# Graph attention on one core: the reference maximum from row tiles 0 to 3, exponents in four groups, source scores negated on the way to PSUM, wh stored in four pieces

## The chip, the cores and the metric

One NeuronCore of a Trainium2 chip runs the whole program in one launch. The metric is the time of one execution on the device in microseconds (us). The core has a matrix engine (PE, TensorE), a vector engine (DVE, VectorE), an activation engine (ACT, ScalarE), a general one (POOL, GpSimd) and SP (SyncE), which here only issues transfers. Each engine runs its own list of instructions in order; engines meet at semaphores.

## The reference, cut to what matters

```
h  = max(layernorm(x), 0);   x1 = x + smooth(adj) @ h        # x: 2048 x 512
h2 = max(layernorm(x1), 0)
Wh = einsum('nf,hfd->hnd', h2, W)                            # 8 heads of 64 columns
e_src = sum(Wh * a1, -1);    e_dst = sum(Wh * a2, -1)        # one score per head and row
e  = leaky_relu(e_src[:, :, None] + e_dst[:, None, :], 0.2)
e  = where(adj > 0, e, -9e15);   att = softmax(e, axis=-1)
h  = elu(att @ Wh);   out = x1 + four dense layers(h)
```

The kernel does not form the exponent of every pair. exp(leaky_relu(s+d)) is one of two products, exp(s)exp(d) or exp(0.2 s)exp(0.2 d), by the sign of s+d. So it multiplies 0/1 matrices by Wh scaled with A = exp(d - top) and C = exp(0.2 (d - top)): q holds the neighbours with d >= -s, mask all neighbours. "top" is the reference maximum per head. That no d lies more than CAP = 40 above it is tested (`safe`); where the test fails, an exact path runs after the normal one.

## The kernel before, in words

The 2048 rows are 16 row tiles of 128. The program has five stages on PE, back to back: smoothing in two halves (to 364.3 us), projection (364.3 to 421.8), attention (to about 797), the dense layers, the end. The change lies in the projection and the first round of attention.

**Projection.** `in_turns` (line 577) gives each engine 16 turns and a few more. At turn k, before the listed stages, an engine does what the code puts under `if k == ...` or in `between(k)`; ACT's extra work is `lead_in(k)` (line 1551), POOL's `lead_in(t)` (line 1718) behind its products of tile t.
- PE at turn k: `turn(k)`, four transposes of the normalised tile, then `project(k-1)`, twelve products into wh. At turns 7 and 12 it first transposes the scores of four tiles (`turn_e`, line 1075). Inside the projection of two tiles stand two small products that spread the maximum (lines 1053, 1056).
- ACT at turn k: `lead_in(k)`, `normalise(k)` (line 741), `cut_turned(k-1)` (line 738: the high part of a turned tile), `take_wh(k-2)` (line 745: wh out of PSUM).
- DVE at turn k: `cut_turned(k)` (line 912: the low part), the maximum and the exponents' arguments, one early tile of q by `choose` (line 1359), `reduce_e(k-2)` (line 915: the scores of a tile from POOL's products).
- POOL: `products(t)` (line 784, two each of 128x512), then its lead-in work.

So a tile goes PE (wh sums), ACT (wh), and the same ACT queue later cuts the tile that PE needs two projections on.

**Preparation of the first head.** `factors` (line 760) makes A and C from args on ACT; `scale_quarter` (line 1544, four instructions) makes C·wh and POOL's `first_product` (line 1704) A·wh for four tiles; `cut_quarter` (line 1535) rounds each to a high part on ACT, `first_rest` (line 1711) subtracts on POOL. The second head's C and A follow as two larger sets (lines 1751 to 1761); its A set waits for `stored` = 48.

**Scores' way.** Transposed scores e_t (16 x 512 for four tiles) go to `e_rows` in HBM and come back broadcast to all partitions in `src` (line 1305, one transfer for each head of the pair); `fill_src` (line 1507) copies them into a PSUM bank, where `choose` compares them with the column neg_d.

**Attention.** Round r handles 512 columns: q phase of the first head (64 products, line 1835), mask phase of both (64, line 1879), q phase of the second head (64). Mask sums leave banks 4, 5, 0 and 1 on ACT (`take_m_sums`, line 1529); the second q phase needs banks 2 to 5. In round 0 `serve` (line 1605) puts `late_factors`, `fill_src(1, 0)` and then `take_m_sums(0)` into ACT's queue.

SP's queue issues in order, and a wait in it holds what follows:

```
for q in range(4):                                            # line 697
    sp.wait_ge(e_copied, q + 1)
    sp.dma_start(e_rows[:, cols], e_t[:, cols])...
    if q == 0: ... first_scores()                             # load_src(0)
sp.wait_ge(stored, 48)
... for r in range(1, LAST + 1): load_src(r)                  # line 1308
```

Of the kernel before, what the change touches and what calls it, by code (L numbers as in the profile page):

```python
# [30 lines left out]
F32 = mybir.dt.float32  # L31
# [10 lines left out]
H = 8  # L42
# [543 lines left out]
def spread_and_project(nc, sems, first, ring, bank, G, rows, rows_loaded, mask, wh, e, fac, args, neg_d, ident, x, adj_t, w,  # L586
                       a1, a2, e_rows, x1_store, in_range):
# [6 lines left out]
    with ExitStack() as ctx:  # L594
# [36 lines left out]
        e_t = rows[0:2 * H, 2:4, :].rearrange("p b n -> p (b n)")  # L631
# [33 lines left out]
        EARLY_Q = 11  # L665
        HALF_TURNS = G8 // SLOTS
        GROUPS = (slice(0, G8), slice(G8, G8 + 4), slice(G8 + 4, T))
# [6 lines left out]
        def sync(sp, first_scores):  # L674
# [93 lines left out]
        def late_factors(a):  # L768
            a.wait_ge(args_ready, 4)
            a.activation(fac["B"][:], args[2][:], ACT.Exp).then_inc(fac_ready, 1)  # L770
            a.wait_ge(args_ready, 5)
            a.activation(fac["D"][:], args[1][:], ACT.Exp).then_inc(fac_ready, 1)
        def late_scores(a, q):
            a.wait_ge(e_turned, q + 1)
            a.wait_ge(e_copied, q)
            a.activation(e_t[:, q * 512:(q + 1) * 512], bank[4 + q % 2][0:2 * H, :], ACT.Copy).then_inc(e_copied, 1)
# [13 lines left out]
        def vector(v, choose_early):  # L790
# [142 lines left out]
            def take_e_t(q):  # L933
                v.wait_ge(e_turned, q + 1)
                v.tensor_copy(e_t[:, q * 512:(q + 1) * 512], bank[4 + q % 2][0:2 * H, :]).then_inc(e_copied, 1)
# [8 lines left out]
            def negate(n):  # L944
                v.tensor_scalar(neg_d[:, GROUPS[n], :], d_m[:, GROUPS[n], :], -1.0, None, ALU.mult).then_inc(chain, 1)
            def exponents(n):
                tiles = GROUPS[n]
                top_t = dst_top[:].to_broadcast([P, tiles.stop - tiles.start, H])
                v.tensor_tensor(args[0][:, tiles, :], d_m[:, tiles, :], top_t, ALU.subtract).then_inc(args_ready, 1)
            def check_range(n):  # L950
                tiles = GROUPS[n]
                v.wait_ge(args_ready, n + 1)
# [1532 lines left out]
```

## Time and profile before

| | us |
|---|---|
| median of 3 runs (lowest to highest) | 865.53 (864.81 to 867.88) |
| the profiled execution: its time / its span | 865.77 / 864.0 |
| PE busy | 842.0 (97% of the span) |
| DVE / ACT / POOL busy | 703.3 / 427.5 / 280.9 |
| granted TensorE clock | full in all 40 slices |

PE's time is 97% of the span, so an engine beside it matters only where PE stands still for it. In 364.3 to 421.8 PE is busy for 57.39 of 57.50 us by the modelled ends of its instructions; those overlap, and how long it stood still is read from the distance of their starts.

### The profile page before, as it was taken

To read this page: it belongs to the slowest core of one execution; us is meant where nothing else is said; L and a number is where in the kernel's file an instruction comes from. 1 tells how busy PE (TensorE), PEld (TensorE's weight loads), DVE (VectorE), ACT (ScalarE), POOL (GpSimd) and SP (SyncE) were. 2 spreads that over 40 slices of the span, in tenths; PEclk is the share of its full clock that TensorE was granted. 3 is DMA by queue.
4 is the path that set the end of the run, shared out by engine and by line. 5 is a ranking of instruction groups with operands and counts; after the bars stand their busy time and mean duration, and the time that the engine had idled before them with its cause. 6 is when DMAs were issued, how large, how long until landed. Compare 5 with 4: busy or idle time off the path is not lost.

```text
span 864.0 us, 15276 instructions
## 1 busy us (share of the span) xinstructions
PE 842.0 (97%) x5207; PEld 757.1 (88%) x5207; DVE 703.3 (81%) x1224; ACT 427.5 (49%) x793; POOL 280.9 (33%) x299
## 2 busy tenths in 40 slices
PE   2999999999999999999999999999999999999998
PEld 2888888888888888887899999999999999999776
DVE  6899886557656885587999999999999999998864
ACT  3445333321111111257766666666666666775753
POOL 0000000000000000066875555555556654566322
PEclk9999999999999999999999999999999999999999
DMA  9979832703223222051340000000000031000134
GB/s 350 406 272 369 354 97 62 205 0 121 97 97 98 97 97 73 1 195 27 130 124 25 16 23 26 26 24 24 26 26 25 24 93 67 25 2 12 39 147 148
DMA packets 37627, 87.97 MB, mean 102 GB/s; under 512 B 7168, under 2 KB 8320, under 8 KB 37568
## 3 DMA queue, kind: packets, MB, share of 16 engines
q1 hardware_dynamic: 35504, 82.98, 27.7%
q10 hardware_dynamic: 2064, 4.26, 1.3%
q8 instruction: 30, 0.49, 0.2%
q14 instruction: 29, 0.24, 0.1%
HBM read 74.45 MB, written 12.78 MB: 101 GB/s over the span
## 4 chain that ended last, share of the span: by engine, by line
PE 92%; DVE 3%; ACT 2%; DMA 2%; issue 1%; POOL 0%; ACTq 0%; DVEq 0%
PE bank L1835 28%; PE bank L77 15%; PE bank L79 14%; PE bank L78 14%; PE bank L1879 14%; PE bank L554 3%; PE bank L2413 1%; PE bank L2407 1%; PE bank L2409 1%; PE bank L2352 1%; DMA l_src<-e_rows 1%; DMA e_rows<-rows 1%; DMA l_h<-x 1%; PE bank L1010 1%; DVE e L915 0%
## 5 line engine op out<-in xcount | busy, mean ns | idle before, releaser
L1359 DVE SCALAR_TENSOR_TENSOR l_q<-bank,neg_d,mask 128x512 fp32r<-128x512 f32 x512 | 339.1, 742 | 23.2 <-PE bank L1835 23.2
L1835 PE MATMUL bank<-l_parts,l_q 128*128 128x260 f32 x2048 | 250.5, 283 | 1.3 <-ACT l_o_m L1533 1.3
L1835 PEld LDWEIGHTS bank<-l_parts,l_q 128*128 128x128 f32 x2048 | 247.0, 188 | 2.3 <-ACT l_o_m L1533 1.6
L77 PE MATMUL bank<-x_hi,s_hi 128*128 128x512 f32 x448 | 174.4, 389 | 0.0
L79 PE MATMUL bank<-x_hi,s_lo 128*128 128x512 f32 x448 | 174.3, 389 | 0.0
L78 PE MATMUL bank<-x_lo,s_hi 128*128 128x512 f32 x448 | 174.3, 389 | 0.0
L784 POOL TENSOR_TENSOR l_prod<-wh,l_a 128x512 f32<-128x512 f32 x29 | 34.0, 1194 | 381.4 <-ACT wh L745 381.4
L1526 ACT ACTIVATE l_o_q<-bank 128x260 f32<-128x260 f32 x128 | 49.0, 388 | 104.7 <-PE bank L1835 97.6
L79 PEld LDWEIGHTS bank<-x_hi,s_lo 128*128 128x128 f32 x448 | 84.1, 188 | 17.6
L78 PEld LDWEIGHTS bank<-x_lo,s_hi 128*128 128x128 f32 x448 | 84.1, 188 | 17.3
L77 PEld LDWEIGHTS bank<-x_hi,s_hi 128*128 128x128 f32 x448 | 84.1, 188 | 17.3
L722 ACT ACTIVATE s_hi<-rows 128x1024 fp32r<-128x1024 f32 x28 | 29.7, 1062 | 122.5 <-PE bank L79 122.5
L1520 ACT ACTIVATE l_mask_near<-mask 128x512 fp32r (+1 forms) x128 | 70.1, 622 | 0.4 <-PE bank L1879 0.3
L1520 ACT ACTIVATE l_mask_far<-mask 128x512 fp32r (+1 forms) x128 | 70.0, 620 | 0.0
L1879 PE MATMUL bank<-l_parts,l_mask_far 128*128 128x260 f32 x512 | 67.7, 284 | 0.0
L1879 PE MATMUL bank<-l_parts,l_mask_near 128*128 128x260 f32 x512 | 67.3, 283 | 0.0
L1879 PEld LDWEIGHTS bank<-l_parts,l_mask_far 128*128 128x128 f32 x512 | 64.6, 189 | 0.0
L1879 PEld LDWEIGHTS bank<-l_parts,l_mask_near 128*128 128x128 f32 x512 | 64.3, 188 | 0.0
L803 DVE CAST x_hi<-G 128x512 fp32r<-128x512 f32 (+1 forms) x32 | 13.6, 425 | 50.7 <-PE bank L79 48.2
L1280 POOL TENSOR_TENSOR l_o_m<-l_o_m 128x520 f32<-128x520 f32 x16 | 18.5, 1159 | 82.7 <-ACT l_o_m L1533 82.7
L808 DVE TENSOR_TENSOR s_lo<-rows,s_hi 128x1024 fp32r<-128x1024 f32 x32 | 39.1, 1223 | 0.2 <-ACT s_hi L722 0.2
L463 ACT ACTIVATE s_hi<-l_now 128x1024 fp32r<-128x1024 f32 x16 | 17.0, 1060 | 39.3 <-PE bank L79 32.3
(229 smaller groups left out, 1190.6 us busy)
## 6 DMA issues: line engine op xcount, KB each, us to landing
rows<-adj_t SPq DMA_DIRECT2D x48, 512.0 KB, 3.7
l_now<-adj SPq DMA_DIRECT2D x16, 512.0 KB, 7.2
l_rows_k<-adj_t SPq DMA_DIRECT2D x16, 512.0 KB, 8.0
l_src<-e_rows SPq DMA_DIRECT2D x32, 256.0 KB, 3.1
l_kept<-adj SPq DMA_DIRECT2D x12, 512.0 KB, 13.1
wh_store<-wh ACTq DMA_DIRECT2D x1, 4160.0 KB, 13.9
l_h<-x SPq DMA_DIRECT2D x4, 1024.0 KB, 17.3
x<-x SPq DMA_DIRECT2D x1, 4096.0 KB, 13.5
```

Source lines behind the costliest of these rows:

```text
L77: pe.matmul(acc, hi, rhs_hi, start=first, stop=False, skip_group_check=True)
L78: pe.matmul(acc, hi, rhs_lo, start=False, stop=False, skip_group_check=True)
L79: return pe.matmul(acc, lo, rhs_hi, start=False, stop=True, skip_group_check=True)
L554: mm = pe.matmul(bank[k][:], left[:, b, k * P:(k + 1) * P], right[:, s, :], start=s == 0 and n == 0, stop=n == 2, skip_group_check=True)
L722: a.activation(a_hi[:, r % 2, :], rows[:, r, :], ACT.Copy).then_inc(hi_ready, 1)
L784: p.tensor_tensor(per_head(prod[:, b, n, :]), wh[:, t, :, 0:HD], per_head(a_b[:, n, :]), ALU.mult).then_inc(prod_ready, 1)
L808: v.tensor_tensor(a_lo[:, b, :], rows[:, r, :], a_hi[:, b, :].bitcast(F32), ALU.subtract).then_inc(lo_ready, 1)
L1359: v.scalar_tensor_tensor(out=q[:, i, :], in0=bank[S_BANKS[hh]][:], scalar=neg_d[:, i, h:h + 1], in1=mask[:, i, cols], op0=ALU.is_ge, op1=A ...
L1520: a.activation(mask_slot(i), mask[:, i, cols], ACT.Copy).then_inc(m_ready, 1)
L1526: a.activation(o_q[hh][:, t, :], bank[Q_BANKS[hh][t]][:, 0:PW], ACT.Copy).then_inc(q_bank_free, 1)
L1835: return pe.matmul(bank[Q_BANKS[hh][t]][:, 0:PW], q[:, i, t * P:(t + 1) * P], parts[pair_slot][:, i, hh * PW:(hh + 1) * PW], start=i == 0, ...
L1879: return pe.matmul(bank[M_BANKS[t]][:, 0:PW], mask_slot(i)[:, t * P:(t + 1) * P], parts[pair_slot][:, i, BOTH_C], start=i == 0, stop=i == ...
```

## The change

The maximum of d is taken over tiles 0 to 3 (turn 6) in place of 0 to 7 (turn 10), and its two small PE products move from the projections of tiles 9 and 10 to those of 6 and 7. args and with them A and C are made in four groups of four tiles, at DVE's turns 8, 10, 14 and the end. neg_d and the three instructions that filled it go: fill_src writes -s, and choose compares with d itself. The test against CAP was two instructions beside the groups and a reduction; it is now one maximum over tiles 4 to 15 and one comparison in `late_args`. The early tiles of q are made at DVE's turns 11, 12, 14, 15 and ahead of the stages of turn 16, before at turns 11 to 15. ACT loads the table of Exp at turn 7, before at turn 8. wh goes to HBM in four transfers in SP's queue, before in one in ACT's. The last two quarters of e_t have a place of their own; `load_src(1)` is issued after the second quarter is stored.

```diff
-        EARLY_Q = 11
+        EARLY_Q = {11: 0, 12: 1, 14: 2, 15: 3, T: 4}
-        GROUPS = (slice(0, G8), slice(G8, G8 + 4), slice(G8 + 4, T))
+        GROUPS = [slice(4 * n, 4 * n + 4) for n in range(4)]
...
-            for q in range(4):
-                cols = slice(q * 512, (q + 1) * 512)
+            def store_e(q):
                 sp.wait_ge(e_copied, q + 1)
-                sp.dma_start(e_rows[:, cols], e_t[:, cols]).then_inc(stored if q else first_stored, 16)
-                if q == 0:
-                    sp.wait_ge(first_stored, 16)
-                    first_scores()
-            sp.wait_ge(stored, 48)
+                sp.dma_start(e_rows[:, q * 512:(q + 1) * 512], turned_e(q, e_late)).then_inc(stored if q >= 2 else first_stored, 16)
+            store_e(0)
+            sp.wait_ge(first_stored, 16)
+            spread_scores(0)
+            keep_wh(0)
+            keep_wh(1)
+            keep_wh(2)
+            store_e(1)
+            sp.wait_ge(first_stored, 32)
+            spread_scores(1)
+            keep_wh(3)
+            store_e(2)
+            store_e(3)
+            sp.wait_ge(stored, 32)
             sp.wait_ge(x1_stored, 16)
...
+                if k == 7:
+                    a.activation(tmp[:, 0:G8], root[:, 0:G8], ACT.Exp, scale=0.0).then_inc(table_loaded, 1)
                 if k == G8:
                     a.wait_ge(norm_ready, 2)
                     a.wait_ge(x1_done, T)
-                    a.activation(root[:], root[:], ACT.Exp, scale=0.0).then_inc(table_loaded, 1)
...
-            exponents(2)
-            negate(2)
-            check_range(2)
+            exponents(3)
             v.wait_ge(prod_ready, 2 * OWN + 2)
             reduce_part(OWN, OWN % 2, 0)
-            v.wait_ge(chain, 4)
...
-                if k == 12:
+                if k == 11:
                     turn_e(range(4, 8))
...
+                def keep_wh(q):
+                    tiles = slice(q * QUAD, (q + 1) * QUAD)
+                    sp.wait_ge(wh_ready, (q + 1) * QUAD + 2)
+                    sp.dma_start(wh_store[q * QW:(q + 1) * QW, :].rearrange("(t p) f -> p t f", p=P),
+                                 wh[:, tiles, :, :].rearrange("p t h e -> p t (h e)")).then_inc(wh_stored, 16)
...
-                                               scalar=neg_d[:, i, h:h + 1], in1=mask[:, i, cols],
-                                               op0=ALU.is_ge, op1=ALU.mult).then_inc(q_ready, 1)
+                                               scalar=e[:, i, H + h:H + h + 1], in1=mask[:, i, cols],
+                                               op0=ALU.is_le, op1=ALU.mult).then_inc(q_ready, 1)
...
-                    if k in (9, 10):
-                        take_mask(0, 0, slice(0, QW), (k - 9,))
+                    if k in (8, 9):
+                        take_mask(0, 0, slice(0, QW), (k - 8,))
+                    elif k == 10:
+                        factors(a, 0)
+                        scale_quarter(0)
                     elif k == 11:
                         fill_src(0, 0)
-                    elif k == 13:
-                        factors(a, 0)
-                        scale_quarter(0)
-                    elif k == 14:
                         a.wait_ge(x1_stored, 16)
                         cut_quarter(0, 1)
+                    elif k == 12:
+                        factors(a, 1)
+                        cut_quarter(0, 0)
+                        take_mask(0, 0, slice(0, QW), (2,))
+                    elif k == 13:
                         scale_quarter(1)
-                    elif k == 15:
-                        cut_quarter(0, 0)
+                    elif k == 14:
                         cut_quarter(1, 1)
+                        cut_quarter(1, 0)
+                        take_mask(0, 0, slice(0, QW), (3,))
                     elif k == 16:
-                        cut_quarter(1, 0)
-                        take_mask(0, 0, slice(0, QW), (2,))
-                    elif k == 17:
-                        factors(a, 1)
+                        factors(a, 2)
                         scale_quarter(2)
...
+                        if hp == 0 and r == 0:
+                            a.wait_ge(stored, 32)
                         if more:
                             a.wait_ge(whole_ready, r + 1)
...
-                p.wait_ge(first_stored, 16)
+                p.wait_ge(first_stored, 32)
+                p.wait_ge(fac_ready, 8)
...
-                p.wait_ge(stored, 48)
                 p.tensor_tensor(second_a, wh[:, :, 1, :], fac["A"][:, :, 1:2].to_broadcast([P, T, HE]),
```

On ScalarE, around the first factors and the scaling of wh for tiles 0 to 3, the queue before reads (wh is a tile's projection, rows the normalised tile, x_hi the high part of a turned tile):

```order
L745 ACTIVATE wh<-bank 128x8x64
L1507 ACTIVATE bank<-l_src 128x512
L741 ACTIVATE rows<-x,l_nmr,l_rstd 128x512
L738 ACTIVATE x_hi<-bank 128x512
L745 ACTIVATE wh<-bank 128x8x64
L741 ACTIVATE rows<-x,l_nmr,l_rstd 128x512
L738 ACTIVATE x_hi<-bank 128x512
L745 ACTIVATE wh<-bank 128x8x64
L763 ACTIVATE fac_A<-args 128x64
L764 ACTIVATE fac_C<-args 128x64
L1548 ACTIVATE l_first_c<-wh,fac_C 128x65 x4
L741 ACTIVATE rows<-x,l_nmr,l_rstd 128x512
```

and the same stretch, turns 10 to 12, in the changed program:

```order
L756 ACTIVATE wh<-bank 128x8x64
L775 ACTIVATE fac_A<-args 128x32
L776 ACTIVATE fac_C<-args 128x32
L1558 ACTIVATE l_first_c<-wh,fac_C 128x65 x4
L752 ACTIVATE rows<-x,l_nmr,l_rstd 128x512
L749 ACTIVATE x_hi<-bank 128x512
L756 ACTIVATE wh<-bank 128x8x64
L1517 ACTIVATE bank<-l_src 128x512
L1551 ACTIVATE l_parts<-l_first_c 128x4x65
L752 ACTIVATE rows<-x,l_nmr,l_rstd 128x512
L749 ACTIVATE x_hi<-bank 128x512
L756 ACTIVATE wh<-bank 128x8x64
```

The factors and the scaling moved from turn 13 to turn 10, ahead of the copy of the source scores, and a cut to the turn of that copy.

On VectorE, at the end of the projection, the queue before reads (e are scores, args the exponents' arguments, l_q the 0/1 tiles):

```order
L912 TENSOR_TENSOR x_lo<-bank,x_hi 128x512
L1359 SCALAR_TENSOR_TENSOR l_q<-bank,neg_d,mask 128x512
L915 TENSOR_REDUCE e<-l_prod 128x8 x2
L925 TENSOR_TENSOR l_prod<-wh,l_a 128x512
L915 TENSOR_REDUCE e<-l_prod 128x8
L931 COPY e<-bank 128x16
L949 TENSOR_TENSOR args<-e,l_dst_top 128x32
L945 TENSOR_SCALAR neg_d<-e 128x32
L953 TENSOR_SCALAR l_in_range<-args 128x32
L915 TENSOR_REDUCE e<-l_prod 128x8
L1359 SCALAR_TENSOR_TENSOR l_q<-bank,neg_d,mask 128x512 x11
```

and in the changed program:

```order
L924 TENSOR_TENSOR x_lo<-bank,x_hi 128x512
L1369 SCALAR_TENSOR_TENSOR l_q<-bank,e,mask 128x512
L927 TENSOR_REDUCE e<-l_prod 128x8 x2
L1369 SCALAR_TENSOR_TENSOR l_q<-bank,e,mask 128x512
L937 TENSOR_TENSOR l_prod<-wh,l_a 128x512
L927 TENSOR_REDUCE e<-l_prod 128x8
L943 COPY e<-bank 128x16
L960 TENSOR_TENSOR args<-e,l_dst_top 128x32
L927 TENSOR_REDUCE e<-l_prod 128x8
L1369 SCALAR_TENSOR_TENSOR l_q<-bank,e,mask 128x512 x11
```

Two small instructions ahead of the eleven tiles are gone, and one early tile stands behind the reduction of tile 13.

## Rows read from the trace of the kernel before

**Rows 1.** TensorE's timeline, first attention round: start, duration, line, count, [idle before].

```profile
421.81 4.68 PE L1835 MATMUL bank<-l_parts,l_q 128*128 128x260 f32 x36
426.33 0.60 PE L1092 MATMUL bank<-ident,e 128*16 128x128 f32 x4
426.68 4.42 PE L1835 MATMUL bank<-l_parts,l_q 128*128 128x260 f32 x28
430.94 2.12 PE L1879 MATMUL bank<-l_parts,l_mask_near 128*128 128x260 f32 x16
...
438.74 0.40 PE L1835 MATMUL bank<-l_parts,l_q 128*128 128x260 f32 x2
440.48 4.73 PE L1835 MATMUL bank<-l_parts,l_q 128*128 128x260 f32 x36 [1.34 <-ACT l_o_m L1533]
```

**Rows 2.** Chain of waits that ended last: start, duration, what.

```profile
427.74 5.56 DMA e_rows<-rows
433.31 6.13 DMA l_src<-e_rows
...
463.77 15.30 PE bank L1835 x128
```

**Rows 3.** VectorE's timeline at the end of the projection.

```profile
421.09 0.72 DVE L945 TENSOR_SCALAR neg_d<-e 128x32 f32<-128x32 f32 x1
421.73 0.74 DVE L953 TENSOR_SCALAR l_in_range<-args 128x32 f32<-128x32 f32 x1
...
422.99 7.32 DVE L1359 SCALAR_TENSOR_TENSOR l_q<-bank,neg_d,mask 128x512 fp32r<-128x512 f32 x11
```

**Rows 4.** TensorE's timeline in the projection, where a tile's turn or product begins.

```profile
376.46 0.60 PE L1010 MATMUL bank<-ident,rows 128*128 128x128 f32 x4
...
379.67 0.60 PE L1010 MATMUL bank<-ident,rows 128*128 128x128 f32 x4
...
407.26 0.60 PE L1010 MATMUL bank<-ident,rows 128*128 128x128 f32 x4
...
410.63 0.60 PE L1010 MATMUL bank<-ident,rows 128*128 128x128 f32 x4
411.29 0.50 PE L77 MATMUL bank<-l_w_hi,x_hi 128*128 128x512 f32 x1
```

**Rows 5.** ScalarE's timeline in the projection.

```profile
386.89 1.28 ACT L758 ACT_TABLE_LOAD   x1
...
390.41 0.62 ACT L1520 ACTIVATE l_mask_near<-mask 128x512 fp32r<-128x512 uint8 x1
...
404.31 0.25 ACT L763 ACTIVATE fac_A<-args 128x64 f32<-128x64 f32 x1
...
405.72 0.80 ACT L741 ACTIVATE rows<-x,l_nmr,l_rstd 128x512 f32<-128x512 f32 x1
...
407.96 0.41 ACT L1541 ACTIVATE l_parts<-l_first_c 128x260 fp32r<-128x260 f32 x1
408.27 1.06 ACT L1548 ACTIVATE l_first_c<-wh,fac_C 128x65 f32<-128x65 f32 x4
409.23 0.81 ACT L741 ACTIVATE rows<-x,l_nmr,l_rstd 128x512 f32<-128x512 f32 x1
```

**Rows 6.** GpSimd's timeline, projection and first round.

```profile
404.50 2.35 POOL L784 TENSOR_TENSOR l_prod<-wh,l_a 128x512 f32<-128x512 f32 x2 [1.52 <-ACT wh L745]
...
421.08 0.70 POOL L1714 TENSOR_TENSOR l_parts<-l_first_a,l_parts 128x260 fp32r<-128x260 f32 x1
421.74 0.70 POOL L1714 TENSOR_TENSOR l_parts<-l_first_c,l_parts 128x260 fp32r<-128x260 f32 x1
...
433.36 1.97 POOL L1758 TENSOR_TENSOR l_whole<-wh,fac_A 128x1040 f32<-128x1040 f32 x1 [3.31 <-DMA e_rows<-rows]
436.15 2.26 POOL L1739 TENSOR_TENSOR l_parts<-l_whole,l_parts 128x1040 fp32r<-128x1040 f32 x1 [0.82 <-DVE l_parts L1370]
```

**Rows 7.** DMA issues, 360 to 445: tensors, queue, count, size, us to landing.

```profile
x_store<-x SPq DMA_DIRECT2D x1, 4096.0 KB, 12.5
```

More of the change, by code:

```diff
@@ L583, in in_turns, with spread_and_project @@
                 work(k - lag, (k - lag) % 2)
-def spread_and_project(nc, sems, first, ring, bank, G, rows, rows_loaded, mask, wh, e, fac, args, neg_d, ident, x, adj_t, w,
-                       a1, a2, e_rows, x1_store, in_range):
+def spread_and_project(nc, sems, first, ring, bank, G, rows, rows_loaded, mask, wh, e, fac, args, ident, x, adj_t, w,
+                       a1, a2, e_rows, x1_store):
     first_part, first_lo_ready, first_slot_free, first_g_done, ident_made = first
@@ L970, in early_q @@
                     exponents(0)
[L971 removed]
+                if t == 10:
+                    exponents(1)
                 if t == 14:
[L973 to L981 removed]
+                    exponents(2)
+                if t in EARLY_Q:
+                    choose_early(EARLY_Q[t])
+            for k in in_turns(T, (cut_turned, 0), (late_chain, 0), (first_top, 0), (reduce_e, 2)):
+                if k == 6:
+                    v.wait_ge(e_ready, 2 * 4 + 4)
+                    v.tensor_reduce(tile_top[:], d_m[:, GROUPS[0], :].rearrange("p t h -> p h t"), AX_X, ALU.max
+                                    ).then_inc(top_ready, 1)
+                if k == T:
+                    choose_early(EARLY_Q[T])
                 if k == 2:
@@ L1095, in spread_and_project, with attend_and_finish @@
         return ((sync, vector, scalar, gpsimd, tensor), (late_args, last_wh, factors, late_factors, late_scores, last_turns),
-                (wh_summed, wh_ready, e_ready, e_copied), x1_stored, (first_stored, stored), fac_ready, EARLY_Q)
-def attend_and_finish(nc, before, bank, wh, e, mask, ident, adj, e_rows, fac, neg_d, wh_store, x1_store, weights, weight_parts, small, out):
+                (wh_summed, wh_ready, e_ready, e_copied), x1_stored, (first_stored, stored), fac_ready, len(EARLY_Q))
+def attend_and_finish(nc, before, bank, wh, e, mask, ident, adj, e_rows, fac, wh_store, x1_store, weights, weight_parts, small, out):
     with ExitStack() as ctx:
@@ L1506, in fill_src @@
                     a.wait_ge(src_loaded[hh], 16 * (r + 1))
-                    a.activation(bank[S_BANKS[hh]][:], src[:, hh, :], ACT.Copy).then_inc(src_filled, 1)
+                    a.activation(bank[S_BANKS[hh]][:], src[:, hh, :], ACT.Copy, scale=-1.0).then_inc(src_filled, 1)
                 def take_mask(r, quad, cols, tiles=range(QUAD)):
@@ L1581, in _ @@
                 cut_quarter(2, 0)
-                factors(a, 2)
+                factors(a, 3)
                 last_wh(a)
@@ L2455, in build @@
         small = sb("retry", [1, 1], mybir.dt.int32), sb("l5_fine_sum", [P, 1]), sb("l5_safe", [P, 1])
-        in_range = sb("l2_in_range", [P, G8, H])
-        before = spread_and_project(nc, ctx, first, ring, bank, G, rows, rows_loaded, mask, wh, e, fac, args, neg_d, ident,
-                                    x, adj_t, w, a1, a2, e_rows, x1_store, in_range)
+        sb("l2_to_w_hi", [P, G8 * H])
+        before = spread_and_project(nc, ctx, first, ring, bank, G, rows, rows_loaded, mask, wh, e, fac, args, ident,
+                                    x, adj_t, w, a1, a2, e_rows, x1_store)
         smooth.close()
-        attend_and_finish(nc, before, bank, wh, e, mask, ident, adj, e_rows, fac, neg_d, wh_store, x1_store,
+        attend_and_finish(nc, before, bank, wh, e, mask, ident, adj, e_rows, fac, wh_store, x1_store,
                           (w1_t, b1, w2_t, b2, w3_t, b3, w4_t, b4), weight_parts, small, out)
```

110 lines of the change are left out of this document (46 added, 64 removed).

## The prediction

> **What bounds the kernel now.** I read the table of busy times first: PE is busy nearly throughout, so only places where PE itself stands still can be won. Then PE's timeline around the change, then the chain of waits, then the engines that PE waits for. The reader is to see three places.
>
> First, the second q phase. PE issues two of its products at 438.74 and goes on at 440.48 [rows 1]; two products are worth 0.24 (128 take 15.30, so 0.1195 each [rows 2]), so 1.50 us are lost, 1.34 of it named as a wait for ACT's copy of the mask sums. The chain says why that copy was late: the last quarter of the scores is stored in HBM in 5.56 us and only then is the broadcast for round 1 issued, which takes 6.13 and lands at 439.44 [rows 2]. ACT's fill waits for it, and the copy stands behind the fill in ACT's queue.
>
> Second, the first q phase. PE has 64 products (7.65) and four transposes (426.33 to 426.68, 0.35), so 8.00 us; it takes from 421.81 to 430.94, 9.13 [rows 1]. The 1.13 are DVE's: it makes the last eleven tiles of q from 422.99 to 430.31, one in 0.67 [rows 3], and PE takes a tile in 0.48.
>
> Third, the projection. An undisturbed turn is 379.67 - 376.46 = 3.21; the one from 407.26 takes 3.37, and behind the transposes of 410.63 the products start 0.66 later where 0.35 is the usual [rows 1, 4]: 0.16 and 0.31 lost, 0.47 together. From 440.48 on the rounds run at PE's rate, and the change touches nothing there that PE waits for.
>
> **The wait at the second q phase.** The broadcast for round 1 now needs only the second quarter of the scores, copied at turn 13 as before, and SP issues its first half when that is stored. Its second half waits for the copy of the other head's scores at the projection's end and is needed long after. So the fill, ACT's last work ahead of the copy, waits no more. What is late next: the copy itself. In round 0 the mask sums of a column tile end only three to none products before the phase does, so the two banks that PE needs after its first two products must be emptied in about 0.24 to 0.36 us. I take 0.2 of the 1.50 as staying, with bounds of 0 and 0.7 (two instructions of the kind of 0.41 at 407.96 [rows 5], less the cover). Gain 1.3, bounds 0.8 and 1.5.
>
> Behind this wait stands another: PE also wants POOL's low parts of the second head, which POOL ends at 436.15 + 2.26 = 438.41, 0.33 ahead of 438.74 [rows 1, 6]. POOL's large product before them had stood 3.31 us for the store of the scores [rows 6]; that wait goes, so POOL no longer holds up VectorE's rounding in front of it, and the margin holds if PE comes only a few tenths earlier. ACT's new wait for the last stores comes behind the copy; queued behind it are round 1's mask tiles, and the transfers have then had a dozen us.
>
> **The first q phase.** DVE loses the last two small instructions ahead of its eleven tiles: they start at 421.09 and 421.73 [rows 3], 0.64 apart, the second 0.74 long and 0.66 until the next by the overlap of the first: 1.30. It gains one early tile of q behind the reduction of tile 13, 0.67, because turn 13 no longer makes one. It starts later by what the projection loses (0.5, below). So 422.99 - 1.30 + 0.67 + 0.5 = 422.86, and the tiles end 0.13 earlier. PE's own bound, 421.81 + 0.5 + 8.00 = 430.31 for its last start, lies beside DVE's 430.81 (430.94 less 0.13), so DVE stays the limit. Gain 0.13; between 1.13, if DVE is ahead, and a loss of 0.4, if the last arguments are dearer. The comparison with d itself, the negated copy, and the changed test are the same instructions on other operands, or a few on 96 columns or fewer that come behind the eleven tiles where DVE runs ahead of PE: nothing.
>
> The two removed instructions were dear for a reason the rows show: their ends, 421.81 and 422.47, fall within 0.03 of the ends of POOL's 421.08 + 0.70 and 421.74 + 0.70 [rows 3, 6]. The Trainium skill, in "SBUF — State Buffer", Who interferes with whom, says that VectorE and GpSimd share a port pair, that an instruction with two SBUF inputs or in a two-port mode takes it whole, and that whoever comes second is blocked to the end; the trace agrees. By that rule the block could pass to the subtraction for the last exponents, which has two SBUF inputs and now stands alone there, and the phase would gain up to 0.7 less: the loss bound above would be reached, and the time would be some 0.6 higher.
>
> **The projection.** ACT's extra work moves forward. From the end of one tile's products at 407.26 to the start of those two tiles on at 411.29 are 4.03 us, in which ACT's extra work is 409.23 - 407.96 = 1.27; the fixed way (wh, normalise, high part, low part) is 2.76. PE's own work between these is 3.21 + 0.35 = 3.56. So a turn hides 0.80 of extra work on ACT, plus 0.44 where four transposes of scores lie in it, plus what PE lost one turn before [rows 4, 5].
> - Turn 7: the table load of 1.28 and its activation [rows 5], from turn 8. The transposes of turn 7 lie in both intervals: no difference.
> - Turn 10: factors and scaling, 405.72 - 404.31 = 1.41 [rows 5]. At turn 13 they had the transposes as cover; here none: 0.61 lost.
> - Turn 11: the copy of the scores and a cut, about 0.8, with any wait for the broadcast. Cover 0.80 + 0.61 + 0.44, as the transposes of tiles 4 to 7 come one turn forward: nothing lost while that wait stays under 1.0. The wait for x1's store passes at once: it was issued before 376.46 and lands in 12.5 [rows 4, 7], long before turn 11.
> - Turn 12: factors 0.45 (1.41 less the scaling's 409.23 - 408.27 = 0.96), a cut 0.31, a mask tile 0.52 (0.62 less the overlap of 0.10 that the cut shows) [rows 5]: 1.28 against 0.80 + 0.44: 0.04.
> - Turn 13: the scaling, 0.96: 0.12. Turn 14: two cuts and a mask tile, 1.14: 0.22. Turn 16: 1.41, without a normalise of 0.81 [rows 5] in that turn: nothing.
> Sum 0.99 against 0.47: 0.5 lost. Bounds: 0.5 won if everything hides, and 1.5 lost if turns 11 and 16 lose 0.5 each beside. The small products of the maximum only change places, two tiles' projections for two others, and their inputs are ready by a turn. The four stores of wh take the place of one in ACT's queue; in SP's queue they stand ahead of the second quarter's store, whose reader, POOL, comes some ten us later.
>
> **The sum.** 0.13 + 1.3 = 1.4 us off (the projection's loss is in the 0.13). The profiled execution took 865.77 with a span of 864.0; it becomes 864.35 and 862.6. The median lies 0.24 below that execution: 864.1.
>
> **Rivals.** (1) The hollows fill entirely: 1.13 + 1.50 + 0.47 = 3.1 off, 862.4. For it speaks that each is a wait and none PE's work; against, that ACT's work in turns 10 to 14 is bunched. (2) The gain is eaten: ACT's turns cost 1.5, the block passes to the arguments, the copy stays late by 0.7: 865.5. For it, the 0.80 of room against 1.41; against, that three bounds must meet. (3) Slower: GpSimd becomes the bound of the projection. From turn 8 on it does a pair of products (2.35) and a piece of 0.70 in each turn [rows 6], 3.05 and a wake-up of 0.15 in a turn of 3.21. ACT at turn 12 waits for the first piece and at turn 14 for the second, with 1.0 and 0.3 us to spare by these numbers. A slip of a whole turn would stop ACT, and so PE, by 2.2 and 2.9: 5.1 more, 869.2. It decides from 0.3 us of lateness on. Against it: GpSimd still idles 1.52 for wh in the row at 404.50. (4) The change does not do what it says: the maximum over fewer tiles fails the test against 40, and the exact path and the dense layers run again, over 1000 us. Scores of one distribution speak against it.
>
> **How the numbers follow.** Forecast 0.74, (1) 0.09, (2) 0.10, (3) 0.06, (4) 0.01. The range 861.9 to 866.4 reaches from (1) to (2), with the forecast and its bounds between, and adds 0.5 below and 0.9 above, since three runs of one kernel lay between 0.7 below and 2.4 above their median; (3) and (4) stay out. A difference under 0.5%, 4.3 us, cannot be told from none: all that PE loses at the three places is 3.1, so faster gets 0.04, slower 0.04, no difference 0.92.
>
> **What would show it.** Right: no idle of PE at the second q phase above 0.3; the broadcast for round 1 landed before 430 in its first half; eleven tiles on DVE starting near 422.9; a late product at turn 10's tile by about 0.6. Wrong: waits of ACT for GpSimd at turns 12 or 14, PE waiting for the low parts of the second head, or a mask phase that starts after 431.

## The result, and the profile after

| | before | after |
|---|---|---|
| median of 8 runs each, us | 865.95 | 868.62 |
| lowest to highest | 864.81 to 867.88 | 867.79 to 870.08 |
| ratio, 95% interval | | 1.0028 [1.0018, 1.0038] |
| the profiled execution: its time / its span | 865.77 / 864.0 | 870.08 / 868.2 |

The change made the kernel slower by 0.28%. That is under the 0.5% named ahead, but the forecast was 1.4 us faster, and 868.62 lies above the range. Cut at the starts of PE's products, the two profiled executions compare as follows.

| stretch | before | after | difference | forecast |
|---|---|---|---|---|
| turn at 379.67 to the first product of the q phase | 42.14 | 46.02 | +3.88 | +0.5 |
| first q phase | 9.13 | 8.61 | -0.52 | -0.63 |
| mask phase, until the second q phase runs on | 9.54 | 9.01 | -0.53 | -1.3 |
| from there to round 1's q phase | 23.29 | 24.83 | +1.54 | 0 |
| sum | 84.10 | 88.47 | +4.37 | -1.4 |

The sum is that of the profiled execution of after, 1.46 above its own median; where those 1.46 lie, experiment 2 shows. The last column has the projection's loss apart from the gain of 0.13.

TensorE's timeline of after: the turns from 379.58 on, then the first round.

```profile
379.58 0.60 PE L1013 MATMUL bank<-ident,rows 128*128 128x128 f32 x4
...
386.42 0.60 PE L1013 MATMUL bank<-ident,rows 128*128 128x128 f32 x4
...
390.84 0.66 PE L1013 MATMUL bank<-ident,rows 128*128 128x128 f32 x4 [0.62 <-ACT rows L752]
...
395.44 0.60 PE L1013 MATMUL bank<-ident,rows 128*128 128x128 f32 x4
...
398.65 0.60 PE L1013 MATMUL bank<-ident,rows 128*128 128x128 f32 x4
399.54 0.50 PE L77 MATMUL bank<-l_w_hi,x_hi 128*128 128x512 f32 x1 [0.29 <-DVE x_lo L924]
...
402.83 0.60 PE L1013 MATMUL bank<-ident,rows 128*128 128x128 f32 x4
...
406.83 0.66 PE L1013 MATMUL bank<-ident,rows 128*128 128x128 f32 x4
...
410.89 0.60 PE L1013 MATMUL bank<-ident,rows 128*128 128x128 f32 x4
...
425.60 0.96 PE L1848 MATMUL bank<-l_parts,l_q 128*128 128x260 f32 x6
...
434.21 2.12 PE L1892 MATMUL bank<-l_parts,l_mask_near 128*128 128x260 f32 x16
...
443.22 14.00 PE L1848 MATMUL bank<-l_parts,l_q 128*128 128x260 f32 x112 [1.07 <-POOL l_parts L1752]
458.05 2.21 PE L1848 MATMUL bank<-l_parts,l_q 128*128 128x260 f32 x16 [0.83 <-DVE l_q L1369]
```

The row of 379.58 answers to 379.67 of [rows 4], those from 425.60 on to [rows 1]. An undisturbed turn was 3.21. The turn from 386.42 now takes 4.42 and the next 4.60; those from 402.83 and 406.83 take 4.00 and 4.06. At the second q phase two waits stand that before did not have: 1.07 for POOL's low parts and 0.83 for a tile of q from DVE.

ScalarE's timeline of after; 383.60 and 441.88 answer to the table load of [rows 5] and to the copy of the mask sums that PE waited for in [rows 1].

```profile
383.60 1.28 ACT L767 ACT_TABLE_LOAD   x1
...
389.45 0.63 ACT L1530 ACTIVATE l_mask_near<-mask 128x512 fp32r<-128x512 uint8 x1 [2.67 <-DVE l_nmr L860]
...
400.94 0.60 ACT L1517 ACTIVATE bank<-l_src 128x512 f32<-128x512 f32 x1 [1.49 <-DMA l_src<-e_rows]
...
404.89 0.23 ACT L775 ACTIVATE fac_A<-args 128x32 f32<-128x32 f32 x1 [1.34 <-DVE args L960]
...
440.21 0.58 ACT L1517 ACTIVATE bank<-l_src 128x512 f32<-128x512 f32 x1
441.88 1.23 ACT L1543 ACTIVATE l_o_m<-bank 128x260 f32<-128x260 f32 x4 [1.09 <-PE bank L1892]
```

VectorE's and GpSimd's timelines of after, at turn 8 and behind the eleven tiles.

```profile
386.32 0.69 DVE L924 TENSOR_TENSOR x_lo<-bank,x_hi 128x512 fp32r<-128x512 f32 x1 [1.87 <-ACT x_hi L749]
386.93 1.15 DVE L856 TENSOR_SCALAR l_tmp<-l_tmp 128x8 f32<-128x8 f32 x1
388.11 1.11 DVE L858 TENSOR_TENSOR l_rstd<-l_rstd,l_tmp 128x8 f32<-128x8 f32 x1
...
403.71 1.15 DVE L960 TENSOR_TENSOR args<-e,l_dst_top 128x32 f32<-128x32 f32 x1
...
433.32 1.07 DVE L1002 TENSOR_SCALAR args<-args 128x128 f32<-128x128 f32 x1
...
434.43 1.89 DVE L1006 TENSOR_SCALAR args<-args 128x128 f32<-128x128 f32 x1
436.24 4.03 DVE L1369 SCALAR_TENSOR_TENSOR l_q<-bank,e,mask 128x512 fp32r<-128x512 f32 x6
440.19 0.68 DVE L1380 CAST l_parts<-l_whole 128x1040 fp32r<-128x1040 f32 x1
```

```profile
386.86 2.34 POOL L796 TENSOR_TENSOR l_prod<-wh,l_a 128x512 f32<-128x512 f32 x2 [0.85 <-ACT wh L756]
...
403.63 2.33 POOL L796 TENSOR_TENSOR l_prod<-wh,l_a 128x512 f32<-128x512 f32 x2 [1.18 <-ACT wh L756]
...
431.68 2.63 POOL L1752 TENSOR_TENSOR l_parts<-l_o_m,l_parts 128x520 fp32r<-128x520 f32 x2
434.27 1.96 POOL L1771 TENSOR_TENSOR l_whole<-wh,fac_A 128x1040 f32<-128x1040 f32 x1
440.95 2.21 POOL L1752 TENSOR_TENSOR l_parts<-l_whole,l_parts 128x1040 fp32r<-128x1040 f32 x1 [4.73 <-DVE l_parts L1380]
```

And VectorE's timeline of before, the rows of the same four small instructions, which are not among the rows shown ahead.

```profile
385.49 0.63 DVE L844 TENSOR_SCALAR l_tmp<-l_tmp 128x8 f32<-128x8 f32 x1
386.16 0.17 DVE L846 TENSOR_TENSOR l_rstd<-l_rstd,l_tmp 128x8 f32<-128x8 f32 x1
...
430.54 0.23 DVE L1000 TENSOR_SCALAR args<-args 128x128 f32<-128x128 f32 x1
...
430.81 0.22 DVE L1003 TENSOR_SCALAR args<-args 128x128 f32<-128x128 f32 x1
```

Two things are to be seen. **At turn 8**: the table load, moved to 383.60, delays ACT's high part of tile 6, so DVE's cut waits until 386.32. Behind it in DVE's queue stand the last instructions of the late norms, now beside POOL's products of 386.86: 1.15 and 1.11 in place of 0.63 and 0.17. (The 0.63 is not the bare price either: it ends at 386.12, and a pair of POOL's products in before, 2.35 from 383.75 on, at 386.10.) ACT waits 2.67 for the last of the norms (L860), and PE turns the next tile late. **Behind the eleven tiles**: two instructions of the late arguments, 0.23 and 0.22 before, take 1.07 and 1.89. They end within 0.1 of the ends of POOL's instructions at 431.68 (two, 1.3 each) and 434.27. In before POOL stood still there, 3.31 us for the store of the scores [rows 6]. So DVE's next six tiles start at 436.24, its rounding of the second head is late at 440.19, POOL's low parts start behind it and end at 443.16, and PE goes on at 443.22.

The chain of waits of after says the second part itself: it runs over the late arguments and DVE's tiles, where before it ran over the two transfers [rows 2].

```profile
433.40 0.99 DVE args L1002
...
436.24 4.03 DVE l_q L1369 x6
```

The transfers are out of it. DMA issues of after from 425 to 446 (tensors, queue, count, size, median us to landing):

```profile
l_src<-e_rows SPq DMA_DIRECT2D x2, 256.0 KB, 3.4
e_rows<-l_e_late SPq DMA_DIRECT2D x2, 32.0 KB, 2.3
```

### The profile page after: what moved, and what is told of

Its sections match the earlier page's. It is cut to its first block, busy times and chain, and to the rows that moved or that the text cites. A ratio compares the mean times of both kernels' runs of the same rounds, so it can differ in the third digit from the quotient of the medians.

```text
span 868.2 us, 15280 instructions
## 1 busy us (share of the span) xinstructions
PE 843.0 (97%) x5207; PEld 756.6 (87%) x5207; DVE 706.0 (81%) x1221; ACT 427.0 (49%) x795; POOL 281.0 (32%) x299
## 4 chain that ended last, share of the span: by engine, by line
PE 88%; DVE 7%; ACT 2%; DMA 1%; issue 1%; DVEq 0%; ACTq 0%
PE bank L1848 26%; PE bank L77 14%; PE bank L79 14%; PE bank L78 14%; PE bank L1892 13%; DVE l_q L1369 3%; PE bank L554 3%; PE bank L2426 1%; PE bank L2420 1%; PE bank L2422 1%; PE bank L2365 1%; DMA l_h<-x 1%; DMA l_src<-e_rows 1%; DVE x_lo L924 0%; ACT rows L752 0%
## 5 line engine op out<-in xcount | busy, mean ns | idle before, releaser
L1369 DVE SCALAR_TENSOR_TENSOR l_q<-bank,e,mask 128x512 fp32r<-128x512 f32 x512 | 339.0, 740 | 22.7 <-PE bank L1848 22.7
```

What stands on the lines that cost most here:

```text
L1369: v.scalar_tensor_tensor(out=q[:, i, :], in0=bank[S_BANKS[hh]][:], scalar=e[:, i, H + h:H + h + 1], in1=mask[:, i, cols], op0=ALU.is_le, o ...
```

## The experiments

The theory was two causes that add: (a) the table load one turn earlier, by the late norms behind it; (b) the late arguments beside POOL, which no longer waits for the stores. Rivals: the small products of the maximum, ACT's bunched work in turns 10 to 14, and, for the wait that went, the order of the broadcast in SP's queue against the 4 MB store beside it. Ratios are to before, timed beside each kernel on the same chip.

**1. The table load back at turn 8 (x1_load_late).** In after:

```diff
-                if k == 7:
-                    a.activation(tmp[:, 0:G8], root[:, 0:G8], ACT.Exp, scale=0.0)...
                 if k == G8:
                     a.wait_ge(norm_ready, 2)
                     a.wait_ge(x1_done, T)
+                    a.activation(tmp[:, 0:G8], root[:, 0:G8], ACT.Exp, scale=0.0)...
```

> The changed kernel with ScalarE's Exp table load back at turn 8, behind the wait for the second half's norms. Theory N (norms): the load at turn 7 holds the cut of tile 6, VectorE's late norms stand behind it and fall beside GpSimd's products, and ScalarE's turn 8 waits 2.67 us for them; so turns 8 and 9 of TensorE, 4.42 and 4.60 us in the changed kernel, come back to 3.7 or less each, and the time falls from 868.6 to between 866.4 and 867.4 (what is lost at the end of the first q phase stays). Rival B (the prediction's own): the load costs the same at either turn, and the loss is ScalarE's bunched work of turns 10 to 14; then the time stays within 0.4 of 868.6.

867.67, 1.0025 [1.0015, 1.0034]: 0.95 less than after, a little short of what was expected. The turn from 386.65 takes 3.33 again, the next still 4.41, which misses the 3.7. Both waits of the second q phase stay (1.1 and 0.8). By the ratios, whose intervals overlap, this run alone is not told from after; 3 and 4 settle what the load costs.

**2. The late arguments later (x2_args_late).** In after, from behind the eleven tiles to behind five more:

```diff
-                late_args(v, safe)
-                choose(0, 0, 1, slice(0, QW), {6: second_cut})
+                choose(0, 0, 1, slice(0, QW), {5: lambda: late_args(v, safe), 6: second_cut})
```

> The changed kernel with the late arguments (five small VectorE instructions) moved from behind the eleven tiles of q to behind five tiles of the second head's q. Theory P (port): in the changed kernel they stand beside GpSimd's second-head work and two of them take 1.07 and 1.89 us where 0.2 is usual, so TensorE waits 1.07 us for GpSimd's low parts and 0.83 for VectorE's tiles. Moved, they take under 0.4 each, TensorE loses under 0.5 there, and the time falls from 868.6 to between 866.5 and 867.4. Rival: the projection's loss alone sets the time and the waits at the second q phase only change their names; then the time stays within 0.4 of 868.6.

867.06, 1.0019 [1.0010, 1.0028]: 1.56 less than after, as expected. The two instructions take 0.22 and 0.23 again, and both of PE's waits are gone. Its projection is that of after, unchanged, and this execution shows it another way:

```profile
379.46 0.60 PE L1013 MATMUL bank<-ident,rows 128*128 128x128 f32 x4
...
402.73 0.60 PE L1013 MATMUL bank<-ident,rows 128*128 128x128 f32 x4
...
405.94 0.60 PE L1013 MATMUL bank<-ident,rows 128*128 128x128 f32 x4
...
409.14 0.60 PE L1013 MATMUL bank<-ident,rows 128*128 128x128 f32 x4
...
423.86 0.96 PE L1847 MATMUL bank<-l_parts,l_q 128*128 128x260 f32 x6
```

379.46 to 423.86 are 44.40, not 46.02. The turns from 402.73 and 405.94 take 3.21 and 3.20 where after's profile had 4.00 and 4.06, and these 1.65 are the whole of the 1.62 between. In after's profile the copy of the scores waited 1.49 for the broadcast, the next arguments then fell beside POOL (403.71 and 403.63 above), and ACT stood 1.34 for them. In 2 the copy waited 0.63, and the same arguments started 0.44 ahead of POOL's products and took 0.18. These two long turns come in some profiles and not in others (in 10 below they do, and in 6 and 7, where ACT's scaling stands ahead of the copy), and they are about what after's profiled execution lies above its median. So the projection's loss that counts for the median is nearer 44.40 - 42.14 = +2.3, and with it the table's sum is +2.8, against 2.67 between the medians.

**3. Both (x3_both).**

> Both edits: the table load back at turn 8 and the late arguments five tiles later. Theories N and P add up: 864.4 to 865.5, below the kernel before (865.95). If the two are one loss seen twice, it is no lower than the better of the two alone, about 866.5.

865.61, 0.9999 [0.9991, 1.0008], 3.0 less than after: 0.1 above the expected range and even with before, not below it. The causes add (0.95 + 1.56 = 2.5) and a little more; timed beside each other on one chip, 3 is 1.45 below 2 by the load and 2.06 below 1 by the late arguments. PE has no wait at the second q phase. The projection still takes 43.30 from 379.96 on, 1.16 more than before's 42.14, and that eats what the two other stretches give.

**4. Before with the load one turn earlier (x4_before_load_early).** The reverse of 1, put into before: the activation with its load, on eight columns as in after, moved ahead of turn 8's waits, under `if k == 7`.

> The kernel before with one part of the change alone: the Exp table load at turn 7 on eight columns, ahead of the waits. Theory N: ScalarE's turn 8 waits over 1.5 us for the late norms and the time rises from 865.95 by 1.0 to 2.2, to 867 to 868.2. Rival B: no difference, within 0.4 of 865.95.

867.0, 1.0018 [1.0010, 1.0027], so +1.5 by that edit alone; in the profiled execution the projection takes 43.28, 1.14 more than before's. VectorE's and ScalarE's timelines show the same picture as after:

```profile
387.51 1.15 DVE L845 TENSOR_SCALAR l_tmp<-l_tmp 128x8 f32<-128x8 f32 x1
388.70 1.11 DVE L847 TENSOR_TENSOR l_rstd<-l_rstd,l_tmp 128x8 f32<-128x8 f32 x1
```

```profile
390.04 0.81 ACT L741 ACTIVATE rows<-x,l_nmr,l_rstd 128x512 f32<-128x512 f32 x1 [2.67 <-DVE l_nmr L849]
```

**5 to 7. ACT's bunched work and the small products, in 3.** x5: the second small product of the maximum behind the last products of its tile. x6: `scale_quarter(0)` from turn 10 to 11, mask tile 3 from 14 to 15. x7: both.

```diff
-                    if t == 7 and k == 1:
+                    if t == 7 and k == KC - 1:
```
```diff
-                        scale_quarter(0)
                     elif k == 11:
+                        scale_quarter(0)
                         fill_src(0, 0)
```

> The kernel with both edits (table load back at turn 8, late arguments moved), and TensorE's small product that spreads the maximum stands behind the last part of tile 7's projection in place of the second. Theory P (port): VectorE's copy of the maximum takes 0.94 us beside GpSimd's products of tile 6 (0.21 in the kernel before), and the small product waits for it inside tile 7's projection; the turn there takes 4.41 us where 3.21 and 0.31 for the small product are usual. Later by two parts, the wait is covered: that turn takes 3.7 or less and the time falls from 865.61 to 864.6 to 865.2. Rival B: the turn is long by ScalarE's work; then it stays at 4.3 or more and the time within 0.3.

> The kernel with both edits, and ScalarE's work spread: the scaling of tiles 0 to 3 goes from turn 10 to turn 11, ahead of the copy of the source scores, where ScalarE waits 1.00 us for the broadcast; one mask tile goes from turn 14 to turn 15. Theory B (bunching, room of 0.80 in a turn): turn 10's 0.54 of loss goes, turn 11 does not rise above what the wait costs now, and the turns behind 14 lose 0.2 less: 864.7 to 865.2 from 865.61. Rival: VectorE at the end of the first q phase sets the time, and what the projection wins is given back there: within 0.3 of 865.61.

> Both of these: 863.6 to 864.7, below the kernel before (865.5), if the port's and the bunching's losses are separate. If the end of the first q phase takes it back, no lower than 865.2.

865.87 (1.0000 [0.9990, 1.0009]), 865.84 (0.9998 [0.9989, 1.0007]), 866.14 (0.9996 [0.9987, 1.0005]): none is told from 3, and all three expectations fail. In x5 the turn in question still takes 4.30, as its rival, ScalarE's work, had it. Rows of 3, of ScalarE and of TensorE, show that work:

```profile
387.19 1.28 ACT L769 ACT_TABLE_LOAD   x1
...
388.60 0.61 ACT L1528 ACTIVATE l_mask_near<-mask 128x512 fp32r<-128x512 uint8 x1
```

```profile
391.18 0.50 PE L77 MATMUL bank<-l_w_hi,x_hi 128*128 128x512 f32 x1 [0.43 <-DVE x_lo L923]
```

With the load back at turn 8, a mask tile that the change moved there from turn 9 stands behind it, ahead of the normalise and the cut. DVE's low part waits for that cut, and PE starts its products 1.04 behind the transposes of 390.14; in before, with the load but no mask tile in that turn, it was 0.65 (389.72 to 390.37), and 0.35 is usual. No run moved this mask tile back, so its price alone is read from the rows and not shown by a run. In x6 turn 10's loss is gone (397.80 to the transposed scores at 401.00 is 3.20), but the turns from 401.48 and 405.67 take 4.19 and 4.08, with the arguments of the second group 1.15 long beside POOL: won in one turn, given back in the next two.

**8. The broadcast last again (x8_broadcast_last).** In 3, `spread_scores(1)` behind all four stores, the order of before:

```diff
-            sp.wait_ge(first_stored, 32)
-            spread_scores(1)
...
             sp.wait_ge(stored, 32)
+            spread_scores(1)
```

> The kernel with both edits, and in SP's queue the broadcast for round 1 again behind the stores of all four quarters of the scores, as in the kernel before; wh still goes out in four pieces. Theory O (order, the prediction's): the broadcast's place behind the last store made ScalarE's copy late; TensorE waits 1 us or more at the second q phase again and the time rises by about 1.2 to 866.8. Rival C (contention): the store's 5.56 us and the broadcast's 6.13 were long because the one transfer of wh, 4 MB, ran beside them; without it they take about 2.3 and 3.4, the broadcast lands some 2 us ahead of its reader, and the time stays within 0.4 of 865.61.

865.24, 0.9993 [0.9985, 1.0002]: no loss. SP's queue shows when:

```profile
431.06 0.82 SPq L1307 DMA_DIRECT2D l_src<-e_rows  x2
```

Issued at 431.06, behind all stores, it is still in time for the fill at 437.80. So it was not the order in SP's queue.

**9. The small copy off the port (x9_top_off_port).** In 3, the copy that spreads the maximum (0.94 there, beside POOL; 0.21 in before) reads PSUM:

```diff
-                    v.tensor_copy(top_w[:], top[:].to_broadcast([H, P]))
+                    v.tensor_scalar(top_w[:], bank[7][0:H, 0:P], top[:, 0:1], None, ALU.max)
```

> The kernel with both edits, and VectorE spreads the maximum by an instruction that reads PSUM (the maximum of the transposed scores and the top, which is the top) in place of a copy from SBUF. Theory P (port): the copy's 0.94 us are a wait for GpSimd's products; reading PSUM it takes 0.25 or less, VectorE's turn 7 is shorter by 0.7 and TensorE's turn of 4.41 us falls to 3.8 or less; time 864.8 to 865.4 from 865.61. Rival: eight partitions and 128 columns are slow at that place for another reason; then 0.9 stays.

865.0, 0.9994 [0.9985, 1.0003]: in the expected range, but not clear of 3. The instruction falls to 0.34, but the turn from 388.90 stays 4.43, which fails the expectation: what PE waits for there is not this copy but, as in 3, DVE's low part (0.44).

**10. wh in one store again (x10_wh_in_one).** In x8, one transfer of 4160 KB from ACT's queue at the old place:

```diff
-            keep_wh(0) ... keep_wh(3)
+                a.dma_start(wh_store..., wh[:]...).then_inc(wh_stored, 16)      # behind cut_quarter(3, 0)
```

> The kernel with both edits and the broadcast for round 1 behind all stores of scores, with wh stored in one transfer from ScalarE's queue at the place it had in the kernel before. Theory C (contention): the last store and the broadcast take 5 to 6 us each again, the broadcast lands after 439, TensorE waits 1 us or more for the mask sums at the second q phase, and the time rises from 865.24 to 866.2 to 867. Rival: without VectorE's and GpSimd's work of the kernel before in front of it, the broadcast is in time anyway; within 0.4 of 865.24.

868.28, 1.0028 [1.0013, 1.0044], 3.0 more than x8 and above the expected range. ScalarE's fill waits again, until 441.54, and SP's queue shows the broadcast issued later than x8's 431.06:

```profile
435.32 7.21 SPq L1303 DMA_DIRECT2D l_src<-e_rows  x3
```

The stores of 32 KB take 5.3 (median to landing; 1.8 in x8, 5.4 in before), the broadcast 6.1 (3.6 in x8), so it lands just ahead of the fill, whose row names a DVE tile in its place; PE waits 2.2 for the copy. The projection is longer too: 378.92 to 423.50 is 44.58 against x8's 43.26, with long turns where after's profile had them. That lies ahead of the store, issued at 425.72, and is not shown to be its doing, so how the 3.0 divide stays open.

**11. POOL held back (x11_pool_held).** In 1, POOL waits for the late arguments before its large product (`p.wait_ge(args_ready, 6)`).

> The kernel with the table load back at turn 8 and the late arguments at their old place; GpSimd waits for them ahead of its large second-head product, as before it waited there for the stores. Theory P (port): the last of VectorE's five small instructions, 1.89 us in the changed kernel, falls to 0.25, the one beside GpSimd's rests stays near 1; TensorE's waits for GpSimd's low parts and VectorE's tiles (1.09 and 0.80) shrink to under 0.6 together, and the time falls from 867.67 to 866.2 to 867.0. Rival: holding GpSimd back costs what VectorE wins, and the time stays within 0.3 of 867.67.

865.8, 1.0002 [0.9993, 1.0012], 1.87 less than 1 and 0.4 below the expected range: a wait added to POOL makes the kernel faster. Of PE's two waits 0.50 is left, for a tile of DVE. VectorE and GpSimd:

```profile
430.53 1.08 DVE L1001 TENSOR_SCALAR args<-args 128x128 f32<-128x128 f32 x1
...
431.64 0.23 DVE L1005 TENSOR_SCALAR args<-args 128x128 f32<-128x128 f32 x1
```

```profile
431.94 1.97 POOL L1771 TENSOR_TENSOR l_whole<-wh,fac_A 128x1040 f32<-128x1040 f32 x1 [0.43 <-DVE args L1005]
```

The first instruction still lies beside the rests and takes 1.08; the second, with POOL still, 0.23 where 1 had 1.89.

**12. Mask tile 3 a turn later (x12_mask_later).** In x9, `take_mask(..., (3,))` under `elif k == 15`.

> The kernel with both edits, the maximum spread from PSUM, and one of ScalarE's mask tiles at turn 15 in place of 14. If theories P and B hold for these two places, the first q product of TensorE comes 1.0 to 1.3 us earlier than in the kernel with both edits, and the time is 864.2 to 864.9, below the kernel before. If VectorE's eleven tiles at the end of the first q phase set the time, it is 865.2 or more.

864.84, 0.9991 [0.9982, 1.0000]: in the expected range, but 0.16 under x9 is no difference that can be told, and the condition failed. The first q product comes 42.99 behind the turn at 379.60, only 0.31 sooner than 3's 43.30, where 1.0 to 1.3 were expected.

**13. Before with wh in pieces alone (x13_before_pieces).** The four stores in SP's queue, behind the first broadcast and the second store of scores; nothing else.

> The kernel before with one part of the change alone: wh is stored in four pieces from SP's queue, three behind the first broadcast and one behind the second quarter's store; all stores of scores still precede the broadcast for round 1. Theory C (contention): the broadcast lands 2 us or more earlier and ScalarE's copy of the mask sums is no longer late, so TensorE's wait of 1.34 for it falls under 0.3. Theory P (port): GpSimd's large product then starts near 430.1, as its stores are there sooner, beside VectorE's late arguments, which rise from 0.71 together to 1.5 or more; net 864.3 to 865.3 from 865.6. If only C holds, 864.0 to 864.5. The prediction's order theory: no change.

865.91, 0.9997 [0.9988, 1.0006]. The broadcast is in time (the fill starts at 436.17 with no wait), and the gain is eaten at once: an instruction of the late arguments takes 1.88 (0.23 before) beside POOL's product, and PE waits 1.0 for POOL and 0.8 for DVE. Mechanism as expected, size missed.

**14. The negation out as well (x14_pieces_no_neg).** In 13, neg_d and its three instructions out, -s written by the fill.

> That kernel, and the negated column of scores and its three instructions are gone (the copy of the source scores negates, the comparison takes the scores). Theory P: VectorE ends its eleven tiles up to 0.6 earlier and so meets GpSimd's rests and its large product with the late arguments, which take 2 us or more together; the gain of the shorter queue is lost there: 864.4 to 865.5, within 0.4 of the kernel with pieces alone. If the port does not matter: 0.6 to 1.0 lower than that kernel.

865.89, 1.0002 [0.9993, 1.0011]: no difference from 13, as theory P had it, though above its range. The first q phase takes 8.45, against 8.52 in 13, which keeps the negation, and 9.13 in before. The block passed on: with the negation gone the range check takes 0.61, where 13 has 0.17, and ends at 421.50, 0.03 behind POOL's 420.77 + 0.70.

**15. And the late arguments later (x15_pieces_no_neg_args_late).** 14 with the edit of 2.

> That kernel with the late arguments five tiles later. Both theories: the late arguments take under 1.2 together, TensorE loses less than 0.4 at the second q phase, and the time is 863.4 to 864.6, below the kernel before and below the best so far (864.84). If GpSimd's large product is late by it, 865 or more.

863.90, 0.9978 [0.9969, 0.9988]: faster than before by 1.9 us, its interval clear of 1, where after stood at 1.0028. VectorE, GpSimd and TensorE:

```profile
434.15 0.23 DVE L998 TENSOR_SCALAR args<-args 128x128 f32<-128x128 f32 x1
...
434.43 0.22 DVE L1001 TENSOR_SCALAR args<-args 128x128 f32<-128x128 f32 x1
```

```profile
435.99 2.24 POOL L1741 TENSOR_TENSOR l_parts<-l_whole,l_parts 128x1040 fp32r<-128x1040 f32 x1 [3.01 <-DVE l_parts L1374]
```

```profile
439.03 16.23 PE L1837 MATMUL bank<-l_parts,l_q 128*128 128x260 f32 x128
```

The arguments take 0.23 and 0.22, the low parts end at 438.23, ahead of PE's 439.03, and PE enters the second q phase without a wait. The phase takes 16.2, against 15.65 in 3: the chain of waits passes from DVE's tiles to PE for the last 16 products. Lead-in, maximum and groups are those of before; what it takes from the change is wh in pieces and the missing negation. Where the 1.9 lie is seen only in part: the stretch from 379.80 to round 1's q phase is 83.24, 0.86 less than before's, in an execution that lies 0.67 above 15's median. And no run moved the late arguments with the negation kept, so that its going is worth anything is not shown.

## Why the prediction was wrong, point by point

**"Turn 7: the table load ... no difference" failed.** Only ACT's own room in the turn was counted. ACT's cut of tile 6 comes behind the load, DVE's late norms behind DVE's cut of that tile, and ACT's turn 8 behind the norms: a ring over two queues, and the norms land beside POOL's products. Experiment 4 prices it alone at +1.5 in before, 3 against 2 at 1.45, experiment 1 at 0.95 in after.

**"That wait goes, so POOL no longer holds up VectorE's rounding", and the late arguments "nothing", failed.** The wait of 3.31 had been cover: while POOL stood in it, VectorE made the late arguments at 0.23 and 0.22. Without it both run at once, and the rounding comes later than before, not earlier. Moving VectorE away (2, 1.56) or holding POOL back (11, 1.87) gives it back. PE's wait for the low parts was named among the signs of a wrong forecast, but the margin of 0.33 was taken to hold on the strength of a wait that goes.

**The wait at the second q phase** for a transfer went, as forecast: the fill at 440.21 and the copy at 441.88 wait for none. The cause given for it was wrong, so that it went was luck, and of the gain of 1.3 the wait for POOL's low parts left 0.53. The order of the broadcast does not matter (8); the 4 MB store beside it does (10), and storing wh in pieces alone removes the wait (13).

**The first q phase** has the size forecast, -0.52 against -0.63. That the removed instructions gave it is not shown: 13 keeps them and gets 8.52, 14 drops the negation and gets 8.45. In 13 the range check, `l_in_range`, took 0.17 in place of 0.74 [rows 3], beside the same POOL row. The starts differ from POOL's by 0.01 in both, so no sum of durations decides such a pair.

**The projection.** Turn 10's loss came as forecast: 398.65 to 399.54 is 0.89 where 0.35 is usual, so 0.54 against 0.61. Turn 11 was to lose nothing "while that wait stays under 1.0"; in after's profile it was 1.49. Turn 12 lost by arguments that were late and blocked, not by ACT's work. Of what 3 still loses (1.16), 5, 6 and 9 each took away a suspected cause and none gave it back (with 9's and 12's edits together it still takes 42.99). Read turn by turn against before, it is the 0.54 of turn 10, 0.39 at turn 8, for which the sum had no entry and where a mask tile now joins the load, and 0.29 from the last turn's transposes to the first q product; that these would come back is not shown. Why 3 equals before by median stays open, while its stretch to round 1's q phase (379.96 to 463.25, against 379.67 to 463.77) is shorter by 0.81 in one execution each: 3's starts the stretch 0.29 later and takes some 0.4 longer behind it.

**The rule that was weighed.** The block was to pass to the subtraction for the last exponents; it did not (425.00, 0.19, POOL idle from 424.65 on), while in 14, which keeps the range check, it did pass to that. The rule itself, of the Trainium skill, "SBUF — State Buffer", Who interferes with whom, that whoever comes second to the shared port pair is blocked to the end, is what the late arguments and the late norms show: the 1.89 begins 0.16 behind POOL's 1.96 and ends 0.09 behind it. It was applied where instructions went away, not where they, or POOL, moved to.

**Rivals.** None came. Of the second, the gain is eaten, the outcome had the sign; of the three bounds that it needed, only the projection's loss was met and passed. That GpSimd becomes the bound (3) did not happen: in the projection no row of ACT waits for POOL. The wake-up of 0.15 in its sum is not what the rows show: in before POOL's products start 0.07 to 0.08 behind the end of ACT's wh, but for the first pair (0.14).

## What to carry to other kernels

When a wait goes, list what the freed engine will now run beside: a wait may be the cover under which another engine's small instructions are quick, and taking it away moves the cost rather than removing it. When a step moves one turn in an in-order queue, follow it through every queue that waits for the step behind it, not only the room in its own. And try the parts of a bundle alone: here two parts and one shift of five tiles beat both the whole and the kernel before, though which of the two parts counts was not tried.

## What the runs showed of the hardware that was not expected

Two of VectorE's instructions on 128x8 elements took 1.15 and 1.11 beside GpSimd (the second 0.17 in before, where it stood alone), and one on 128x128 took 1.89 in place of 0.22: each lasted until GpSimd's instruction ended, however small it was. An instruction that reads PSUM did the work of an 8x128 copy out of SBUF in 0.34 in place of 0.94 (9). A 32 KB store took 5.2 to 5.6 us beside one store of 4160 KB from ACT's queue (before, 4, 10) and 1.8 to 2.3 where that was cut into four earlier pieces; the broadcast of 256 KB 6.1 to 6.6 against 3.4 to 3.8.
